# A fused graph-and-Mamba kernel: five steps of the graph part reordered, GpSimd's injections and ScalarE's evacuations moved

## What is computed

```python
# layer 1: graph attention and a polynomial in the transition matrix
Xw = X @ Wv + bv                       # X = layernorm(x)
e = leaky_relu(sj[:, None, :] + si[:, :, None] + ab, 0.2)
alpha = A * exp(e)
transition = alpha / (sum(alpha, axis=-1, keepdims=True) + 1e-12)
for k in range(3):
    H = H + Xk @ Wk[k] + bk[k]
    Xk = transition @ Xk
x = x + relu(H)
# layer 2: Mamba block on layernorm(x), 1024 channels, 16 states, 4 conv taps
u = silu(conv4(u) + conv_b)
dt, B_ssm, C_ssm = split(u @ W_xproj.T)
delta = softplus(dt @ W_dt.T + b_dt)
h = exp(delta * A) * h + (delta * u) * B_t        # scan over the 128 rows
y = sum_s(h * C_t) + u * D
x = x + fc2(W_out(y * silu(z)))
```

## Time and profile before

| | us |
|---|---|
| median of 3 runs | 3949.91 |
| range of the runs | 3949.03 to 3950.27 |
| the profiled execution's own time | 3946.52 |
| its span | 3944.4 |
| mean granted clock of TensorE over the span, share of 2.4 GHz | 0.979 |

### The profile page before, as it was taken

How to read it: one execution, slowest core, us unless ns; L and a number is a source line. 1 busy time by engine, 2 the same in 40 slices (tenths; PEclk the granted TensorE clock), 3 DMA queues, 4 the chain that set the end, 5 groups by cost and what they waited for, 6 DMA issues and landing times. The chain is left out here.

```text
span 3944.4 us, 43314 instructions
## 1 busy us (share of the span) xinstructions
PE 3506.4 (89%) x10938; PEld 1931.7 (49%) x10938; DVE 3646.4 (92%) x3133; ACT 2830.4 (72%) x6002; POOL 3451.7 (88%) x1860
## 2 busy tenths in 40 slices
PE   6789899999899999899989899989899899899887
PEld 3545455545455444455444455444455444445443
DVE  0499999999999999999999999999999999999998
ACT  1477777777777877777877777877777777677775
POOL 0298889998889998889998889998889998889999
PEclk9899999999999999999999999999999999999999
DMA  2111101111101111101111101111100111100110
GB/s 106 50 53 56 55 9 50 53 55 55 55 8 50 52 55 55 55 14 45 53 55 55 55 16 42 52 55 55 55 21 37 53 55 55 55 26 28 49 49 8
DMA packets 50715, 183.77 MB, mean 47 GB/s; under 512 B 7340, under 2 KB 33204, under 8 KB 42068
## 3 DMA queue, kind: packets, MB, share of 16 engines
q1 hardware_dynamic: 48880, 174.17, 11.5%
q10 hardware_dynamic: 1636, 7.83, 0.5%
HBM read 164.15 MB, written 17.83 MB: 46 GB/s over the span
## 5 line engine op out<-in xcount | busy, mean ns | idle before, releaser
L407 POOL TENSOR_TENSOR st<-st,bc 128x1024 f32<-128x1024 f32 x1024 | 2399.2, 2360 | 310.6 <-DVE st L843 310.5
L843 DVE TENSOR_TENSOR_SCAN st<-dec,st 128x1024 f32<-128x1024 f32 x1024 | 2310.0, 2277 | 26.6 <-ACT dec L460 20.3
L668 PE MATMUL y_ps<-st,ident 128*128 128x512 f32 x4096 | 1984.9, 613 | 309.7 <-POOL st L407 308.3
L460 ACT ACTIVATE dec<-delta,decay 128x254 f32<-128x254 f32 x4096 | 1696.8, 467 | 623.6 <-DVE st L843 608.3
L668 PEld LDWEIGHTS y_ps<-st,ident 128*128 128x128 f32 x4096 | 745.1, 192 | 1178.9 <-issue 582.2
L831 DVE TENSOR_TENSOR st<-du,bc 128x1024 f32<-128x1024 f32 x736 | 884.6, 1202 | 4.0 <-ACT du L446 4.0
L398 POOL TENSOR_TENSOR st<-du_sb,bc 128x1024 f32<-128x1024 f32 x288 | 679.5, 2360 | 0.1
L869 DVE SCALAR_TENSOR_TENSOR u<-d_ps,chan,u 128x250 f32<-128x250 f32 (+2 forms) x768 | 308.7, 472 | 68.1 <-ACT u L500 68.0
L706 PE MATMUL d_ps<-xnT,wxz 128*128 128x256 f32 x1024 | 250.5, 388 | 55.5 <-DVE u L869 55.5
L706 PEld LDWEIGHTS d_ps<-xnT,wxz 128*128 128x128 f32 x1024 | 191.0, 191 | 157.0 <-DVE u L869 107.1
L718 PE MATMUL d_ps<-xnT,wxz 128*128 128x256 f32 x1024 | 247.3, 385 | 13.6 <-ACT zs L509 13.5
(11 more groups left out here) (98 smaller groups left out, 2452.4 us busy)
## 6 DMA issues: line engine op xcount, KB each, us to landing
bc<-bc_dram SPq DMA_DIRECT2D x64, 2048.0 KB, 9.5
xg<-x_dram SPq DMA_DIRECT2D x32, 256.0 KB, 11.4
x_dram<-xg SPq DMA_DIRECT2D x32, 256.0 KB, 2.0
last_x<-x_dram SPq DMA_DIRECT2D x32, 256.0 KB, 2.6
out_dram<-last_x SPq DMA_DIRECT2D x32, 256.0 KB, 2.2
bc<-w_inT_dram ACTq DMA_DIRECT2D x1, 4096.0 KB
adjt<-adjT_dram SPq DMA_DIRECT2D x32, 128.0 KB, 11.1
bc<-w_out_dram ACTq DMA_DIRECT2D x1, 2048.0 KB
```

Of the source, the lines that this page charges most:

```text
L407: nc.gpsimd.tensor_tensor(st[:, sl, :, :, :], st[:, sl, :, :, :], bc[:, p, 1, SU * q:SU * q + SU, None, :].to_broadcast([P, SU, 2, T]), AL ...
L460: a = nc.scalar.activation(dec[:, v % 2, s, j, :].rearrange("p (b t) -> p b t", b=PAIR)[:, :, 1:], delta[:, p, 2 * i + j, :].rearrange("p ...
L668: mm = nc.tensor.matmul(y_all, ident[:, :], st[:, sl, s, :, :].rearrange("p j t -> p (j t)"), start=False, stop=(q == Q - 1 and s == SU - ...
L843: nc.vector.tensor_tensor_scan(h, dec[:, v % 2, :, :, :].rearrange("p s j t -> p (s j t)"), h, 0.0, ALU.mult, ALU.add).then_inc(S["scanned ...
```

## The change

Three things are changed together.

1. **GpSimd's work.** Its nine injections move to units 0, 2, 4, 6, 8, 10, 15, 20 and 26; step sizes and inputs come earlier; two injections of the next pair (0 and 2) are made at the end of a round instead of one. `du_sb` has two buffers.
2. **Row sums.** PE makes the row sums as two one-column products, so that they stand as 128x2. DVE adds the constant and takes the reciprocal on 128x2. ScalarE scales the identity by each reciprocal (two activations of 128x128 into `xn`), PE multiplies a matrix of ones by them, which spreads the reciprocals over the partitions, and DVE multiplies alpha by that. To fit, x2k and the logits change places.
3. **Evacuation of u.** It moves from `dense_act`, behind the decays of v+1, to ahead of them in units 1, 3, 5, 7.

```diff
-POOL_UNITS = (0, 4, 8, 12, 16, 20, 24, 27, 30)
-POOL_INJECTS = {0: 4, 5: 8, 8: 12, 12: 16, 16: 20, 20: 24, 23: 27, 26: 30}
-POOL_DELTAS = {2: 1, 9: 2, 14: 3}
-POOL_DUS = {4: 1, 11: 2, 18: 3}
-NEXT_DELTA, NEXT_DU, NEXT_INJECT = 27, 28, 29
+POOL_UNITS = (0, 2, 4, 6, 8, 10, 15, 20, 26)
+POOL_INJECTS = {1: 4, 3: 6, 5: 8, 7: 10, 11: 15, 16: 20, 22: 26}
+POOL_DELTAS = {0: 1, 2: 2, 6: 3}
+POOL_DUS = {2: 1, 9: 2, 17: 3}
+NEXT_DELTA, NEXT_DU, NEXT_INJECTS = 27, 28, {29: 0, 31: 2}
...
-        du_sb = sb("du_sb", [P, 2, T])
+        du_sb = sb("du_sb", [P, 2, 2, T])
+        rowsum = sb("rowsum", [P, PAIR])
+        rinv = sb("rinv", [P, PAIR])
...
 def step_input(pool, g, r, i):
                 wait(pool, "delta_made", JP * g + i + 1)
-                wait(pool, "du_copied", JP * g + i)
-                wait(pool, "p_injected", NP * g + pool_before(Q * i))
-                nc.gpsimd.tensor_tensor(du_sb[:, :, :], ...
+                wait(pool, "du_copied", JP * g + i - 1)
+                wait(pool, "p_injected", NP * g + pool_before(Q * (i - 1)) if i else NP * (g - 1) + pool_before(Q * (JP - 1)))
+                nc.gpsimd.tensor_tensor(du_sb[:, i % 2, :, :], ...
...
 ScalarE, body:
                 for v in range(U):
+                    if dense and v - 1 in U_STEPS:
+                        evacuate_u(act, k + 1, r, U_STEPS.index(v - 1))
                     if scan and v + 1 < U:
                         decays(act, k, p, v + 1)
...
 ScalarE, graph_act: xn at 33 also waits for rinv_mm; x2k copy 11 -> 18; exponentials 14 -> 11; x1k copy 24 -> 25
+                if v == 17:
+                    wait(act, "rinv_made", g + 1)
+                    for b in range(PAIR):
+                        a = nc.scalar.activation(xn[:, b, 0:P], ident[:, :], ACT.Copy, scale=rinv[:, b:b + 1])
+                    a.then_inc(S["rinv_diag"], 1)
...
 PE, graph_pe: x2k product 9 -> 16 (waits for rinv_made); logits 12 -> 9; x1k 21, 22 -> 22, 23; h 25, 26 -> 26, 27
-                if v == 17:
+                if v == 14:
                     wait(pe, "alpha_made", g + 1)
-                    nc.tensor.matmul(g0[:, 0:T], ones[:, :], att[:, :, :].rearrange("p b i -> p (b i)"), ...
+                    for b in range(PAIR):
+                        mm = nc.tensor.matmul(g0[:, b:b + 1], att[:, b, :], ones[:, 0:1], start=True, stop=True)
+                if v == 19:
+                    wait(pe, "x2k_made", g + 1)
+                    wait(pe, "rinv_diag", g + 1)
+                    for b in range(PAIR):
+                        mm = nc.tensor.matmul(g0[:, b * L:(b + 1) * L], ones[:, :], xn[:, b, 0:P], start=True, stop=True)
+                    mm.then_inc(S["rinv_mm"], 1)
...
 DVE, graph_dve: alpha 15 -> 12; x1 28 -> 29
-                if (v, late) == (19, 1):
+                if (v, late) == (15, 1):
                     wait(dve, "rowsum_mm", g + 1)
-                    nc.vector.tensor_scalar(g0[:, 0:T], g0[:, 0:T], EPS_ROW, None, ALU.add)
+                    nc.vector.tensor_scalar(rowsum[:, :], g0[:, 0:PAIR], EPS_ROW, None, ALU.add)
                     wait(dve, "rowsum_eps", g + 1)
-                    nc.vector.reciprocal(g0[:, T:2 * T], g0[:, 0:T])
+                    nc.vector.reciprocal(rinv[:, :], rowsum[:, :])
+                if (v, late) == (20, 1):
+                    wait(dve, "rinv_mm", g + 1)
                     nc.vector.tensor_tensor(att, g0[:, 0:T], att, ALU.mult)
```

More of the change, by code:

```diff
@@ L397, in inject @@
                 wait(pool, "summed", U * g + v + 1 - SLOTS)
-                nc.gpsimd.tensor_tensor(st[:, sl, :, :, :], du_sb[:, None, :, :].to_broadcast([P, SU, 2, T]),
+                nc.gpsimd.tensor_tensor(st[:, sl, :, :, :], du_sb[:, i % 2, None, :, :].to_broadcast([P, SU, 2, T]),
                                         bc[:, r, 0, SU * q:SU * q + SU, None, :].to_broadcast([P, SU, 2, T]),
@@ L445, in copy_du @@
                 wait(act, "injected", ND * k + dve_before(Q * i))
-                nc.scalar.activation(du[:, :, :], du_sb[:, :, :], ACT.Copy).then_inc(S["du_copied"], 1)
+                nc.scalar.activation(du[:, :, :], du_sb[:, i % 2, :, :], ACT.Copy).then_inc(S["du_copied"], 1)
             def decays(act, k, p, v):
@@ L488, in finish, with evacuate_u @@
                 nc.scalar.activation(last_x[:, :, :], o_ps[:, :, :], ACT.Copy).then_inc(S["finished"], 1)
-            def dense_act(act, g, r, v):
[L491 to L501, removed]
+            def evacuate_u(act, g, r, i):
+                wait(act, "u_mm", J // 2 * g + i + 1)
+                wait(act, "summed", U * (g - 2) + Q * (i + 1))
+                if isinstance(g, int) and g == 0 and i == 0:
+                    act.wait_ge(S["bias_loaded"], 16)
+                    act.wait_ge(S["bconv_made"], 1)
+                for j in (2 * i, 2 * i + 1):
+                    nc.scalar.activation(u[:, r, j, :], d_ps[:, j % 2, :], ACT.Identity, bias=bconv[:, j:j + 1],
+                                         scale=chan[:, TAPS - 1, j:j + 1]).then_inc(S["u_biased"], 1)
+            def dense_act(act, g, r, v):
                 if v - 1 in Z_STEPS:
@@ L545, in graph_act @@
                     wait(act, "transposed", 2 * g + second)
+                    if second:
+                        wait(act, "rinv_mm", g + 1)
                     for b in range(PAIR):
@@ L563, in graph_act @@
                         .then_inc(S["e_exp"], 1)
-                if v == 24:
+                if v == 25:
                     wait(act, "x1k_mm", g + 1)
@@ L755, in graph_pe @@
                     mm.then_inc(S["transposed"], 1)
-                if v == 9:
-                    wait(pe, "xT_made", g + 1)
+                if v == 16:
+                    wait(pe, "rinv_made", g + 1)
                     for b in range(PAIR):
@@ L761, in graph_pe @@
                     mm.then_inc(S["x2k_mm"], 1)
-                if v == 12:
-                    wait(pe, "x2k_made", g + 1)
+                if v == 9:
+                    wait(pe, "xT_made", g + 1)
                     for b in range(PAIR):
@@ L786, in graph_pe @@
                         mm.then_inc(S["x1k_mm"], 1)
-                if v in (25, 26):
-                    b = v - 25
+                if v in (26, 27):
+                    b = v - 26
                     wait(pe, "x1k_made", g + 1)
@@ L918, in graph_dve @@
                     a.then_inc(S["aggr"], 1)
-                if (v, late) == (15, 1):
+                if (v, late) == (12, 1):
                     wait(dve, "e_exp", g + 1)
```

28 lines of the change are left out of this document (13 added, 15 removed).

## The result

| | before | after |
|---|---|---|
| median, us | 3949.47 (4 runs) | 3888.72 (4 runs) |
| range, us | 3947.16 to 3950.27 | 3887.83 to 3890.40 |
| profiled span, us | 3944.4 | 3886.1 |
| mean granted clock over the span | 0.979 | 0.970 |

What follows compares the result with a forecast made beforehand. DVE was taken to bound the kernel: 111.4 us of work plus 3.2 of waits made a 114.6 us round against 118.1; 98, 3 and 10 us saved gave 111, so 3839 us, range 3785 to 3905.

Steps and rivals of the forecast that it cites:

- the walk: Timeline of the engines' queues through one changed round; with DVE's work it gave 3.2 us of waits, round 114.6.
- c(6): GpSimd's c of unit 6 ends 32.0 us into the round; PE runs through from there.
- first taps: DVE's wait ahead of the round's first taps stays at 0.9 + 0.08 us, since both sides moved.
- scan 5: New DVE wait of 0.6 us (0 to 1.2), as ACT's x1k copy comes behind silu of z and delays decays 5.
- injection 16: New DVE wait of 0.7 us at unit 15: the copy of du stands behind dbc on ACT, done at 57.2.
- the signs that were named: Right if DVE busy near 111.8, no 256-column reciprocals, taps waiting once, a `copy_du` wait under 1 us, c(6) at 32 us.
- signs of being wrong: Gates waiting for PE ahead of scan 10, the product with alpha waiting for PE, or `copy_du` waiting over 2 us.
- the term for the clock: Behind c(6), a fall to 1.2 GHz costs 1.7 to 3.4 us at injection 16; a quarter counted, 0.5 us.
- the gate before scan 18: DVE's wait there goes: c(15) ends at 63.2, its sum at 65.7, gate at 68.3; saves 1.7 us.
- GpSimd's queue is 1 injection shorter at the end: In the last three rounds, with less dense or graph work, this and DVE's savings of 4, 4 and 2 give 10 us.
- PE at 1.2 GHz in every round: Rival, chance 0.17: GpSimd's early-loaded queue holds PE back, c(6) to dbc loses 2.5 us; round 116.7, 3901 us.
- Slower through the copy: Rival, chance 0.08: DVE's injection 16 waits for ACT's copy behind dbc; round 119.2, 3980 us.

Runs made afterwards that it cites:

- the filler run: The changed kernel with the second of the four step-size projections made three times over, 2.1 us more useless PE work a round: 3887.03 us.
- the last round's own list: The changed kernel with GpSimd's injections of the last round alone at the old places, one fewer: 3880.48 us.

## Why the prediction was right, and where it was off

**Right.** The direction, and the walk that gave it. c(6), summed by PE from 1715.75 (31.8 us into the round), was put at 32.0. dbc was copied at 56.3 into the round and the copy of du ended at 57.2, both as predicted to 0.1 us; DVE's work a round came to 111.2 (111.4). The first taps, scan 5, injection 16 and scan 27 wait at their places. The chain on two columns costs 0.14 and 0.17 us for constant and reciprocal, 0.35 foretold. GpSimd's c and injections last 2.36 us in the mean, as in the earlier trace rows, although GpSimd is at work during nearly all of the taps, as it was before, so adding nothing for that was right. The Trainium skill ("SBUF — State Buffer", Who interferes with whom) says that a DVE instruction with two SBUF inputs contends with a GpSimd instruction that reads SBUF. A tap takes 0.47 us with GpSimd at work beside it and 0.48 without, so its per-partition scalar in SBUF doesn't count as a second input. Of the signs that were named, DVE's 111.5 us of work in a round, the taps that wait once and the end of c(6) came out right. But two waits of L851 for `copy_du` came instead of one; in rounds 8 and 10 the second is over 2 us, and in rounds 3 and 17 the product with alpha waits 0.8 us for PE. Both had been named as signs of being wrong.

**Off: the term for the clock.** I priced the fall at 0.5 us a round, at the stretch behind c(6), where the kernel before shows it. In the changed kernel PE idles 1.51 us there and the clock holds in all 28 rounds. It falls at 69 us, behind a wait that the change itself made: with the gate before scan 18 no longer waiting for PE, PE waits for the gate. I had removed DVE's wait from the sum (its sum at 65.7, the gate at 68.3) without asking what PE would do from 65.7 to 68.3. The cost lands on `copy_du` for unit 24, which I had not walked in the text at all: 0.94 us a round, 26 us in all. The rounds without the fall come near the forecast, but only the odd ones: 114.2 to 114.5, while even ones without it, seen in the filler run, take 115.3 or more.

**Off: the last three rounds.** "GpSimd's queue is 1 injection shorter at the end" gave -10 us; measured +6.2. The placement is made for a round with taps. Without taps DVE runs ahead of injections 4, 6 and 8 (7 us), and 2.4 us more pass before the first scan. Together with the clock term this is most of the 50 us that are missing.

**Off by less.** Scan 5 waits 0.95 instead of 0.6, scan 27 0.62 instead of 0.4, and in every second round injection 1 waits for its slot. One scaled identity took 393 ns, not 300.

**The rivals.** "PE at 1.2 GHz in every round" had the right kind of cause, a low clock that delays the copy of du. Its place (behind c(6)), who holds PE back (GpSimd; it is DVE's gate) and its price (2.1 us a round more than the forecast, against 0.94) were off. That its 3901 us lies near the measured 3888.7 is luck: about a third of what the forecast missed is before the first round and in the last three, which the rival had not touched. "Slower through the copy" names the very instruction that pays, one block earlier; GpSimd's order alone turned it into a loss of 44 us, with the copy for unit 16 late by 2.0 us in one kind of round and that for unit 24 by 3.0 in the other. That this part, and the row sums too, lose alone was outside everything I had considered: I had costed the three parts as a sum with one walk, and the walk was of all three.

**Open.** What makes the clock fall at 69 us isn't settled. A shorter wait of PE went with fewer falls (9 of 28 with 1.09 us, 24 with 2.20), yet with 0.5 us, the rest filled by products of 32 rows, 22 rounds fell. Filling with full 128-row products wasn't tried.

## What to carry to other kernels

When a change takes away a wait of the engine that sets the pace, look at once at the engine that it waited for: it will now wait itself, its clock may fall, and what stands behind it in its queue pays. Undo and add parts separately before crediting any of them: here two losing parts and one winning part made the gain, and the cheapest repairs (a gate ahead of an injection, 25 us; the last round's own list, 8 us) lay in none of them. A placement tuned for the steady round should be walked once more for the rounds that lack part of the work.

## What the runs showed of the hardware

- Moving 1.3 us of matmuls by one unit changed the time by 46 us, since it decides whether TensorE's clock is at 1.2 or 2.4 GHz during one sum (3.66 against 1.98 us for the same four matmuls; the fall came in 27 of 28 rounds behind a wait of 2.64 us, in none behind 1.35). The Trainium skill ("TensorE: Matmul & The Clock Gate", Part 1) names the throttled clock as the default that activity lifts; these rows agree.
- The clock can fall in one round and hold in the next with the same instructions and the same wait ahead (0.49 and 0.50 us in the filler run; 2.20 to 2.25 in all 28 rounds of the changed kernel, 24 with the fall), so a trace of one round doesn't show what a kernel pays.
- A VectorE constant on 128x2 from PSUM takes 137 ns and a reciprocal of 128x2 166 ns in the mean; a ScalarE copy of 128x128 with a per-partition scale 393 ns.
